# Turns before diagonal products in self-attention, and two row sends moved across a block's end

## The chip, the core and the metric

The kernel runs on one NeuronCore of a Trainium2 chip. The core has TensorE (matrix products; the profile shows its products as PE and its weight loads as PEld), VectorE (DVE), ScalarE (ACT), GpSimd (POOL) and SyncE (SP, which here only issues DMAs). The engines run side by side, each in the order of its own program, and meet on semaphores. The metric is the time of one execution on the device in microseconds (us), lower is better.

## The reference

A decoder layer over x of 32 batches x 100 tokens x 256 features, in float32, cut to what matters:

```python
x = x + attn(layernorm(x), wq, wk, wv, wo)        # 16 heads of 64, softmax over 100 keys, no mask
x = x + xattn(layernorm(x), context, mask, ...)   # 16 heads of 16, 361 keys
x = x + ffn(layernorm(x), centroids, w1, w2, ...) # 8 experts, one for each token

# self-attention, per head: the projection is *reshaped* to (heads, tokens, 64), not transposed
scores = softmax(q @ k.T * 64 ** -0.5)
out = (scores @ v).reshape(tokens, 1024) @ wo.T

# experts: eid = argmax(x @ centroids.T)
y = x + relu((xhat * gamma[e] + beta[e]) @ w1[e] + b1[e]) @ w2[e] + b2[e]
out = alpha * y + (1 - alpha) * x                 # alpha = sigmoid(x @ centroids[e])
```

## The kernel before

Four blocks follow each other: constants, self-attention (to 637 us), cross-attention (to some 1222 us) and the experts. A block ends when every engine has drained and met a barrier; GpSimd's drain and the barrier carry the line on which the block was opened or entered (L161 for self-attention, L847 for cross-attention).

**Self-attention.** Eight quads of four batches. A quad first projects queries, keys and values (the "body", TensorE lines L64 to L66), then runs eight rounds, r = 0 to 7, and three more (r = 8, 9, 10) in which the pipeline empties and the next quad's first projections are put between. A round takes two groups g of four heads, one of each of two batches. The softmax needs a maximum per query, so each score is computed twice. In round r TensorE does, in this order:

- L747: scores of round r, queries on the rows (4 loads), only for their maxima. VectorE reduces them to `row_max` (L634), GpSimd makes of each group's maxima a negative diagonal matrix `diag` (L541).
- L765: products of `probs` with the values for the groups of round r - 2 (16 loads, into `ps_o` and `ps_p`). `probs` is the weight operand, so the load itself waits for ScalarE's exponentials. VectorE then divides by the sums (L642, L646, `o_norm`).
- L787: scores of round r - 1 with the keys on the rows (16 small products into `ps_t`).
- L791: for each of the two groups one product of ones with `diag`, which subtracts the maxima in `ps_t` and completes it. ScalarE takes the exponentials after it (L454, `probs`).
- L801: four transposes, "turns", of `o_norm` of round r - 2 into `ps_ot`. ScalarE copies them out (L464, `stage`), GpSimd splits them in a high and a low part (L529 `o_hi`, L531 `o_lo`).
- after the fourth and the eighth round of outputs (in r = 6 and r = 10) the output products of two batches, 48 products on L64 to L66 that read `o_hi` and `o_lo` and wait for the last `o_lo`.

ScalarE's order in round r is: exponentials of round r - 1 (L454, each waits for its group's L791), copies of the turned outputs of round r - 2 (L464, wait for the turns of both groups), then the casts of the operands of round r + 2 (L275, L428). GpSimd's order in round r: the split of the outputs of round r - 3 (L529, L531), then the diagonals of round r, two of them, each of which may overwrite its buffer only after the L791 of the same buffer one round before. VectorE's: maxima, then `recip` and `o_norm` of the two groups, then the cast L275.

**The seam.** Cross-attention ends with the routing of the tokens to experts. Each batch's rows go to their places in `routed_rows` by an indirect DMA that GpSimd issues. For the last five batches (`LAST = 5`, batches 27 to 31) `send_last_rows` (L1225 to L1233) does it straight from `x`, by `last_slots`, which VectorE fills. In the end GpSimd does, for n = 29, 30, 31, `add_counts(n)` (L1196) and `send_last_rows(n - 1)`, then the send of batch 31, then waits for all landings (`routed`, L1295); SyncE waits for them as well (L1135), after it has issued the rows and weights of the experts' tiles 0 and 1.

**The experts.** 20 tiles of 256 or 128 rows. For tile 0: VectorE takes moments (L2195, L2199), GpSimd the roots (`roots(0)`, L2121 to L2125), VectorE `xhat` (L2206) and `feats` (L2211), GpSimd the sum `xf` (`residual(0)`, L2133), TensorE turns `xhat` (L2275), ScalarE makes `h_in` (L2167), TensorE the two layers (L2295, L2306). SyncE loads a tile's rows (L2032) and weights (L2037, L2038) two tiles ahead; the first that it loads in this block is tile 2, whose weights go to `w_third`. GpSimd scatters finished rows (L2140).

Of the kernel before, what the change touches and what calls it, by code (L numbers as in the profile page):

```python
# [25 lines left out]
GH = 4  # L26
# [24 lines left out]
HALVES = (2, 2, 2, 1) + (2, 2, 1) * 2 + (2, 1) * 5  # L51

EARLY_BATCHES = B - 6
EARLY = -(-(S * EARLY_BATCHES - E * (T - 1)) // T)
MAXT = (B * S + T - 1) // T
REGION = MAXT * T
# [98 lines left out]
def self_attention(nc, c, x, wqkT, wvT, woT, v_dram, xs, cross):  # L155
# [5 lines left out]
    with ExitStack() as ctx:  # L161
# [516 lines left out]
        def _(pe):  # L678
# [30 lines left out]
            def quad(q, last):  # L709
# [24 lines left out]
                for r in range(-1, ROUNDS + TAIL):  # L734
# [49 lines left out]
                    for h in range(GH):  # L784
                        for g in pair:

                            pe.matmul(ps_t[g % 2][0:S, S * h:S * (h + 1)], head(k_t, g, h), head(q_t, g, h),  # L787
                                      start=(h == 0), stop=False, skip_group_check=True)
                    for g in pair:
                        pe.wait_ge(diag_ready, q * GQ + (g + 1))  # L790
                        pe.matmul(ps_t[g % 2][0:S, 0:GH * S], c.ones_r[0:S, 0:S],  # L791
                                  diag[:, g % 2].rearrange("p h j -> p (h j)"), start=False, stop=True,
                                  skip_group_check=True).then_inc(shifted_ready, 1)
                    for g in in_round(r - 2):
                        pe.wait_ge(o_ready, q * GQ + (g + 1))
                        if g == 0:
                            reach(pe, x1_ready, q * QUAD)
                        if g >= 2:
                            pe.wait_ge(ot_copied_act, q * 2 * GQ + 2 * (g - g % 2))
                        for w in range(2):  # L800
                            ins = pe.transpose(ps_ot[:, 2 * S * (g % 2) + S * w:2 * S * (g % 2) + S * (w + 1)],  # L801
                                               o_norm[:, g % 2, 128 * w:128 * (w + 1)], c.ident[0:S, 0:S])
                        ins.then_inc(ot_ready, 1)
                    for g in in_round(r - 3):
                        if last_round_of_pair(r - 3):
                            i = batch_of(g)
                            pe.wait_ge(o_lo_ready, q * ROUNDS + (r - 2))
                            if i >= 2:
                                pe.wait_ge(x1_ready, q * QUAD + 2)
                            if isinstance(q, int) and q == 0:  # L810
                                pe.wait_ge(vo_lo_ready, 4)
                            hi, lo = (t[:, i % 2] for t in (o_hi, o_lo))
                            wo_hi, wo_lo = (w[:, 3].rearrange("p k n -> p (k n)").rearrange(
                                "p (t n) -> p t n", n=D) for w in (w_hi, w_lo))
                            for t in range(NT):
                                ins = split3(pe, ps_y[i // 2][0:S, D * (i % 2):D * (i % 2 + 1)], hi[:, t, :],
                                             lo[:, t, :], wo_hi[:, t, :], wo_lo[:, t, :], t == 0, t == NT - 1)
                            ins.then_inc(y_ready, 1)
# [14 lines left out]
def cross_attention(nc, c, ctxT, wo, bo, kb_dram, kd, qd, ones_dram, centT, xs, moe):  # L833
# [13 lines left out]
    with ExitStack() as ctx:  # L847
# [7 lines left out]
            return ctx.enter_context(nc.semaphore(name))  # L855

        KP = KT[0]
        LAST = 5
        wq_sb, wk_st, wv_st, wo_sb = c.wq_sb, c.wk_st, c.wv_st, c.wo_sb
        bq_sb, bk_sb, bv_sb, bo_sb, key_live = c.bq_sb, c.bk_sb, c.bv_sb, c.bo_sb, c.key_live  # L860
        wk_hi = sb("wk_hi", [128, KD, D], F32R)
# [46 lines left out]
        slot_f = sb("slot_f", [S, 1])  # L908
        slot = sb("slot", [S, 2], U32)
        last_f = sb("last_f", [S, 1])  # L910
        last_slots = sb("last_slots", [S, LAST], U32)
        ps_p = [psum(f"psb_p{i}", [128, 512]) for i in range(2)]
        ps_s = [psum(f"psb_s{i}", [128, 512]) for i in range(2)]
        ps_t = [psum(f"psb_t{i}", [128, 512]) for i in range(2)]
# [64 lines left out]
        counts_ready = sem("counts_ready")  # L979
        placing = sem("placing")  # L980
        slot_ready = sem("slot_ready")
        routed = [sem(f"routed{p}") for p in range(2)]
        last_placing = sem("last_placing")

        K0, Q0, K1, MT1, RT, V0, MT0, V1, V2, XT = range(10)
# [59 lines left out]
        def _(sp):  # L1045
# [85 lines left out]
            load_weights(sp, c, 0, c.w1_sb[:, 0], c.w2_sb[:, 0], moe["w1"], moe["w2"])  # L1131
            load_rows(sp, c, 1, xs)
            load_weights(sp, c, 1, c.w1_sb[:, 1], c.w2_sb[:, 1], moe["w1"], moe["w2"])
            for p in range(2):
                sp.wait_ge(routed[p], 16 * (B // 2))  # L1135

        @block.gpsimd
        def _(pool):
# [86 lines left out]
            def send_last_rows(n):  # L1225

                pool.wait_ge(slot_ready, n + 1)
                if n < EARLY_BATCHES + 2:
                    pool.wait_ge(routed[n % 2], 16 * (EARLY_BATCHES // 2))
                pool.indirect_dma_start(  # L1230
                    out=xs, out_offset=bass.IndirectOffsetOnAxis(ap=last_slots[:, n - (B - LAST):n - (B - LAST) + 1],
                                                                 axis=0),
                    in_=c.x[:, n, :], in_offset=None).then_inc(routed[n % 2], 16)  # L1233

            def routing(b, p):

# [52 lines left out]
            routing_root(B - 1)  # L1289
            for n in range(B - 3, B):  # L1290
                add_counts(n, n % 2)
                send_last_rows(n - 1)
            send_last_rows(B - 1)
            for p in range(2):
                pool.wait_ge(routed[p], 16 * (B // 2))  # L1295

        @block.scalar
        def _(act):
# [585 lines left out]

def table_buffers(nc, c, ctx):

    c.totals = ctx.enter_context(nc.sbuf_tensor("totals", [1, 2, E], F32))
    c.steps = ctx.enter_context(nc.sbuf_tensor("steps", [1, 3, MAXT], F32))
    c.tile_no = ctx.enter_context(nc.sbuf_tensor("tile_no", [1, BIG], F32))
# [142 lines left out]
    sp.dma_start(c.rows[:, j % 3, 0:nh], src).then_inc(c.rows_loaded[j % 3], 16)  # L2032


def load_weights(sp, c, j, w1_dst, w2_dst, w1, w2):
    e = expert_of(sp, c, j)
    sp.dma_start(w1_dst, w1[bass.ds(e, 1)].rearrange("o (k p) n -> p (o k) n", p=128)).then_inc(c.w_loaded[j % 3], 16)  # L2037
# [3 lines left out]
def experts(nc, c, xs, w1, w2, out):  # L2041
# [4 lines left out]
    with ExitStack() as ctx:  # L2046
# [56 lines left out]

        @block.sync
        def _(sp):
            for j in range(TILES - 2):
                if j + 2 == EARLY:
                    sp.wait_ge(c.tiles_ready, 6)
# [7 lines left out]
        def _(pool):  # L2116
# [26 lines left out]
                        oob_is_err=False).then_inc(scattered[j % 4], 16)  # L2143

            roots(0)
            residual(0)
            for j in range(TILES):
                if j + 1 < TILES:
# [252 lines left out]
```

## Time and profile before

| | |
|---|---|
| median of 3 runs | 1476.35 us (1476.33 to 1479.77) |
| the profiled execution | 1477.7 us, its span 1475.8 us, mean granted TensorE clock 0.977 |
| PE busy | 1372.4 us, 93% of the span |
| PEld busy | 1192.2 us, 81% |
| DVE / ACT / POOL busy | 950.5 (64%) / 761.4 (52%) / 651.4 us (44%) |
| DMA | 217.44 MB, mean 147 GB/s |
| self-attention, cross-attention, experts | 0 to 637, 637 to 1224.6, 1224.8 to 1475.8 us |

The span is the time from the first to the last instruction of the profiled execution; the device time has a little around it. A busy TensorE isn't one at its peak: products are pipelined and the ends of those in the profile are modelled, so the weight loads (PEld) show better when TensorE moves on. A row of the timeline gives start, length, engine, line, operation, output<-inputs, shapes and count; what stands in square brackets is the idle time of that engine before the row and the instruction that ended it. A q behind an engine's name marks its sequencer (waits, barriers, DMA issue).

### The profile page before, as it was taken

How to read it: one execution, taken by the hardware profiler on the slowest of the kernel's cores; microseconds unless marked ns; L12 is line 12 of the kernel's file. 1: busy time of each engine (PE TensorE's matmuls, PEld its weight loads, DVE VectorE, ACT ScalarE, POOL GpSimd, SP SyncE). 2: the span in 40 equal slices, each digit the busy share in tenths (PEclk: the TensorE clock that was granted, in tenths of full speed). 3: DMA queues.
4: the chain of work that ended last, by engine and by line, in shares of the span. 5: the costliest groups of instructions: out<-in, count | busy, mean ns of one | idle time of the engine just before them, and what ended most of it. 6: DMA issues, size and time to landing. Idle time of an engine off the chain costs nothing. (4 is left out here: it accounts for less than half of the span.)

```text
span 1475.8 us, 39048 instructions
## 1 busy us (share of the span) xinstructions
PE 1372.4 (93%) x12162; PEld 1192.2 (81%) x12162; DVE 950.5 (64%) x2409; ACT 761.4 (52%) x1882; POOL 651.4 (44%) x1001
## 2 busy tenths in 40 slices
PE   6999999999999999859999999999999976999997
PEld 5888888887878787847888888888888865888887
DVE  5757575757575666436777777777777754655554
ACT  5747474746565565514665656565565631222222
POOL 5534344352626171732345555555555541333332
PEclk9999999999999999978999999999999987999999
DMA  6607162524334252537767777677766652666662
GB/s 195 156 1 169 30 145 51 127 69 107 89 85 111 66 130 59 141 103 206 190 176 193 192 194 187 176 193 192 196 187 175 178 189 82 227 214 215 209 220 70
DMA packets 181116, 217.44 MB, mean 147 GB/s; under 512 B 83486, under 2 KB 148933, under 8 KB 180774
## 3 DMA queue, kind: packets, MB, share of 16 engines
q1 hardware_dynamic: 176424, 209.60, 52.2%
q0 software_dynamic: 3584, 6.58, 1.4%
q8 instruction: 44, 0.72, 0.2%
q10 hardware_dynamic: 1024, 0.21, 0.1%
q14 instruction: 40, 0.33, 0.1%
HBM read 137.62 MB, written 79.43 MB: 147 GB/s over the span
## 5 line engine op out<-in xcount | busy, mean ns | idle before, releaser
L1478 DVE TENSOR_REDUCE row_max<-psb_s 100x1 f32<-100x361 f32 x512 | 265.5, 530 | 143.5 <-PE psb_s L1694 137.8
L1348 ACT ACTIVATE probs<-psb_t 121x400 f32<-121x400 f32 (+1 forms) x384 | 190.5, 508 | 88.3 <-PE psb_t L1704 82.2
L541 POOL TENSOR_TENSOR diag<-neg_ident,row_max 100x400 fp32r<-100x400 f32 x128 | 112.9, 903 | 260.0 <-DVE row_max L634 231.3
L1694 PE MATMUL psb_s<-k,q 97*100 97x362 f32 x512 | 185.2, 364 | 15.3 <-DVE row_max L1478 7.7
L1704 PE MATMUL psb_t<-q,k 98*121 98x200 f32 (+1 forms) x768 | 146.4, 273 | 1.7 <-ACT probs L1348 1.7
L1704 PEld LDWEIGHTS psb_t<-q,k 98*121 98x121 f32 (+1 forms) x768 | 125.7, 184 | 4.5 <-ACT probs L1348 2.4
L454 ACT ACTIVATE probs<-ps_t 100x400 f32<-100x400 f32 x128 | 57.5, 501 | 113.2 <-PE ps_t L791 113.2
L1694 PEld LDWEIGHTS psb_s<-k,q 97*100 97x100 f32 x512 | 85.8, 168 | 35.5 <-DVE row_max L1478 18.0
L2181 ACT ACTIVATE hid<-psd_h,b_sb 128x256 f32<-128x256 f32 (+1 forms) x100 | 43.2, 432 | 113.7 <-PE psd_h L2295 113.6
L1717 PE MATMUL psb_o<-probs,v_ext 121*32 121x100 f32 (+1 forms) x3072 | 92.8, 253 | 0.0
L309 ACT COPY q_t<-ps_p 64x200 f32<-64x200 f32 x112 | 57.4, 512 | 63.6 <-PE ps_p L66 62.8
L529 POOL CAST o_hi<-stage 128x400 fp32r<-128x400 f32 x64 | 59.9, 937 | 62.0 <-ACT stage L464 33.5
L634 DVE TENSOR_REDUCE row_max<-ps_s 100x4 f32<-100x400 f32 x128 | 67.5, 570 | 28.7 <-PE ps_s L747 28.2
L2295 PE MATMUL psd_h<-h_in,w_sb 128*128 128x256 f32 (+1 forms) x448 | 83.1, 343 | 2.6 <-ACT h_in L2167 1.4
L464 ACT COPY stage<-ps_ot 64x200 f32<-64x200 f32 x256 | 81.7, 319 | 6.1 <-PE ps_ot L801 1.2
L64 PE MATMUL ps_p<-x_lo,w_hi 128*128 128x400 f32 x224 | 81.1, 362 | 4.0 <-DVE q_t L309 0.2
L531 POOL TENSOR_TENSOR o_lo<-stage,o_hi 128x400 fp32r<-128x400 f32 x64 | 81.7, 1277 | 5.1
L2295 PEld LDWEIGHTS psd_h<-h_in,w_sb 128*128 128x128 f32 x448 | 73.1, 195 | 11.7 <-DVE hid L2241 1.9
L1717 PEld LDWEIGHTS psb_o<-probs,v_ext 121*32 121x32 f32 (+1 forms) x3072 | 64.4, 110 | 21.4 <-issue 15.5
L2306 PE MATMUL psd_y<-w_sb,hid 128*128 128x256 f32 x352 | 80.4, 379 | 0.0
L66 PE MATMUL ps_p<-x_hi,w_hi 128*128 128x400 f32 x224 | 77.3, 345 | 0.0
L65 PE MATMUL ps_p<-x_hi,w_lo 128*128 128x400 f32 x224 | 76.9, 343 | 0.0
(255 smaller groups left out, 3738.1 us busy)
## 6 DMA issues: line engine op xcount, KB each, us to landing
w_sb<-in_w SPq DMA_DIRECT2D x28, 1024.0 KB, 7.5
routed_rows<-empty SPq DMA_DIRECT2D x7, 3855.0 KB, 19.8
packed_keys<-k_st SPq DMA_DIRECT2D x32, 724.0 KB, 4.4
k<-packed_keys SPq DMA_DIRECT2D x64, 362.0 KB
v_rows<-v_tok SPq DMA_DIRECT2D x32, 400.0 KB
v_ext<-v_rows SPq DMA_DIRECT2D x32, 400.0 KB
q<-packed_queries SPq DMA_DIRECT2D x64, 200.0 KB
w_third<-in_w SPq DMA_DIRECT2D x12, 1024.0 KB, 7.7
```

Source lines behind the costliest of these rows:

```text
L64: pe.matmul(out, hi_l, lo_r, start=first, stop=False)
L66: return pe.matmul(out, hi_l, hi_r, start=False, stop=last)
L464: act.copy(*turned_part(r - 2, a, odd)).then_inc(ot_copied_act, 1)
L531: pool.tensor_tensor(lo, src, hi.bitcast(F32), ALU.subtract).then_inc(o_lo_ready, 1)
L541: pool.tensor_tensor(diag[:, g % 2], c.neg_ident[0:S, 0:S].unsqueeze(1).to_broadcast([S, GH, S]), row_max[:, g // 2 % 2, g % 2].unsqueeze( ...
L1348: act.activation(probs[0:KT[kt], u % 2, kt], ps_t[i % 2][0:KT[kt], 0:4 * S], ACT.Exp, scale=HD2 ** -0.5).then_inc(probs_ready, 1)
L1478: dve.reduce_max(row_max[:, p, h:h + 1], ps_s[h % 2][0:S, 0:S2], AX_X).then_inc(max_ready, 1)
L1694: pe.matmul(ps_s[h % 2][0:S, 0:S2E], q2[0:97, p, u, g, S * a:S * (a + 1)], k2[0:97, p, u, g], start=True, stop=True).then_inc(scores_ready, 1)
L1704: ins = pe.matmul(ps_t[i % 2][0:n, 2 * S * g:2 * S * (g + 1)], k2[:, p, u, g, rows], q2[:, p, u, g], start=True, stop=True)
L1717: ins = pe.matmul(ps_o[32 * h:32 * (h + 1), S * u:S * (u + 1)], v_ext[0:n, p, kt, 4 * u + h, :], probs[0:n, u % 2, kt, S * h:S * (h + 1)], ...
L2295: ins = pe.matmul(ps_h[f % 4][:, 0:UNIT * nh], w1_sb[j % 3][:, k, 128 * f:128 * (f + 1)], h_in[:, j % 2, k, 0:UNIT * nh], start=(k == 0), ...
L2306: ins = pe.matmul(ps_y[n % 3][:, 0:D], hid[:, f, UNIT * t:UNIT * (t + 1)], w2_sb[j % 3][:, f, :], start=(f == 0), stop=(f == NF - 1))
```

## The change

Two parts. In self-attention the loop over the turns (L801) is placed ahead of the loop over the diagonal products (L791) in TensorE's program; nothing else of the round moves. At the seam the sends of batches 30 and 31 are taken out of the cross-attention block, with the waits for all landings on GpSimd and SyncE at its end; GpSimd issues them in the experts' block, after `roots(0)` and before `residual(0)`, and SyncE waits for all landings at the head of the experts' block, before it loads the rows of tile 2. `last_slots` and the two `routed` semaphores are allocated outside the block for that.

```diff
--- before.py
+++ after.py
@@ -51,6 +51,8 @@
 HALVES = (2, 2, 2, 1) + (2, 2, 1) * 2 + (2, 1) * 5
 
 EARLY_BATCHES = B - 6
+
+LAST = 5
 EARLY = -(-(S * EARLY_BATCHES - E * (T - 1)) // T)
 MAXT = (B * S + T - 1) // T
 REGION = MAXT * T
@@ -786,11 +788,6 @@
 
                             pe.matmul(ps_t[g % 2][0:S, S * h:S * (h + 1)], head(k_t, g, h), head(q_t, g, h),
                                       start=(h == 0), stop=False, skip_group_check=True)
-                    for g in pair:
-                        pe.wait_ge(diag_ready, q * GQ + (g + 1))
-                        pe.matmul(ps_t[g % 2][0:S, 0:GH * S], c.ones_r[0:S, 0:S],
-                                  diag[:, g % 2].rearrange("p h j -> p (h j)"), start=False, stop=True,
-                                  skip_group_check=True).then_inc(shifted_ready, 1)
                     for g in in_round(r - 2):
                         pe.wait_ge(o_ready, q * GQ + (g + 1))
                         if g == 0:
@@ -801,6 +798,11 @@
                             ins = pe.transpose(ps_ot[:, 2 * S * (g % 2) + S * w:2 * S * (g % 2) + S * (w + 1)],
                                                o_norm[:, g % 2, 128 * w:128 * (w + 1)], c.ident[0:S, 0:S])
                         ins.then_inc(ot_ready, 1)
+                    for g in pair:
+                        pe.wait_ge(diag_ready, q * GQ + (g + 1))
+                        pe.matmul(ps_t[g % 2][0:S, 0:GH * S], c.ones_r[0:S, 0:S],
+                                  diag[:, g % 2].rearrange("p h j -> p (h j)"), start=False, stop=True,
+                                  skip_group_check=True).then_inc(shifted_ready, 1)
                     for g in in_round(r - 3):
                         if last_round_of_pair(r - 3):
                             i = batch_of(g)
@@ -855,7 +857,6 @@
             return ctx.enter_context(nc.semaphore(name))
 
         KP = KT[0]
-        LAST = 5
         wq_sb, wk_st, wv_st, wo_sb = c.wq_sb, c.wk_st, c.wv_st, c.wo_sb
         bq_sb, bk_sb, bv_sb, bo_sb, key_live = c.bq_sb, c.bk_sb, c.bv_sb, c.bo_sb, c.key_live
         wk_hi = sb("wk_hi", [128, KD, D], F32R)
@@ -908,7 +909,7 @@
         slot_f = sb("slot_f", [S, 1])
         slot = sb("slot", [S, 2], U32)
         last_f = sb("last_f", [S, 1])
-        last_slots = sb("last_slots", [S, LAST], U32)
+        last_slots = c.last_slots
         ps_p = [psum(f"psb_p{i}", [128, 512]) for i in range(2)]
         ps_s = [psum(f"psb_s{i}", [128, 512]) for i in range(2)]
         ps_t = [psum(f"psb_t{i}", [128, 512]) for i in range(2)]
@@ -979,7 +980,7 @@
         counts_ready = sem("counts_ready")
         placing = sem("placing")
         slot_ready = sem("slot_ready")
-        routed = [sem(f"routed{p}") for p in range(2)]
+        routed = c.routed
         last_placing = sem("last_placing")
 
         K0, Q0, K1, MT1, RT, V0, MT0, V1, V2, XT = range(10)
@@ -1131,8 +1132,6 @@
             load_weights(sp, c, 0, c.w1_sb[:, 0], c.w2_sb[:, 0], moe["w1"], moe["w2"])
             load_rows(sp, c, 1, xs)
             load_weights(sp, c, 1, c.w1_sb[:, 1], c.w2_sb[:, 1], moe["w1"], moe["w2"])
-            for p in range(2):
-                sp.wait_ge(routed[p], 16 * (B // 2))
 
         @block.gpsimd
         def _(pool):
@@ -1227,10 +1226,7 @@
                 pool.wait_ge(slot_ready, n + 1)
                 if n < EARLY_BATCHES + 2:
                     pool.wait_ge(routed[n % 2], 16 * (EARLY_BATCHES // 2))
-                pool.indirect_dma_start(
-                    out=xs, out_offset=bass.IndirectOffsetOnAxis(ap=last_slots[:, n - (B - LAST):n - (B - LAST) + 1],
-                                                                 axis=0),
-                    in_=c.x[:, n, :], in_offset=None).then_inc(routed[n % 2], 16)
+                send_rows_of(pool, c, n, xs)
 
             def routing(b, p):
 
@@ -1289,10 +1285,8 @@
             routing_root(B - 1)
             for n in range(B - 3, B):
                 add_counts(n, n % 2)
-                send_last_rows(n - 1)
-            send_last_rows(B - 1)
-            for p in range(2):
-                pool.wait_ge(routed[p], 16 * (B // 2))
+                if n < B - 1:
+                    send_last_rows(n - 1)
 
         @block.scalar
         def _(act):
@@ -1884,6 +1878,8 @@
 
 def table_buffers(nc, c, ctx):
 
+    c.last_slots = ctx.enter_context(nc.sbuf_tensor("last_slots", [S, LAST], U32))
+    c.routed = [ctx.enter_context(nc.semaphore(f"routed{p}")) for p in range(2)]
     c.totals = ctx.enter_context(nc.sbuf_tensor("totals", [1, 2, E], F32))
     c.steps = ctx.enter_context(nc.sbuf_tensor("steps", [1, 3, MAXT], F32))
     c.tile_no = ctx.enter_context(nc.sbuf_tensor("tile_no", [1, BIG], F32))
@@ -2032,6 +2028,13 @@
     sp.dma_start(c.rows[:, j % 3, 0:nh], src).then_inc(c.rows_loaded[j % 3], 16)
 
 
+def send_rows_of(pool, c, n, xs):
+
+    at = n - (B - LAST)
+    pool.indirect_dma_start(out=xs, out_offset=bass.IndirectOffsetOnAxis(ap=c.last_slots[:, at:at + 1], axis=0),
+                            in_=c.x[:, n, :], in_offset=None).then_inc(c.routed[n % 2], 16)
+
+
 def load_weights(sp, c, j, w1_dst, w2_dst, w1, w2):
     e = expert_of(sp, c, j)
     sp.dma_start(w1_dst, w1[bass.ds(e, 1)].rearrange("o (k p) n -> p (o k) n", p=128)).then_inc(c.w_loaded[j % 3], 16)
@@ -2103,6 +2106,8 @@
 
         @block.sync
         def _(sp):
+            for p in range(2):
+                sp.wait_ge(c.routed[p], 16 * (B // 2))
             for j in range(TILES - 2):
                 if j + 2 == EARLY:
                     sp.wait_ge(c.tiles_ready, 6)
@@ -2143,6 +2148,8 @@
                         oob_is_err=False).then_inc(scattered[j % 4], 16)
 
             roots(0)
+            for n in (B - 2, B - 1):
+                send_rows_of(pool, c, n, xs)
             residual(0)
             for j in range(TILES):
                 if j + 1 < TILES:
```

## Rows read from the trace of the kernel before

**Rows 1.** Waits, 80 to 600 us: engine line waited for: us in total, times, longest.

```profile
PEld ps_o L765 <- ACT probs L454: 3.6, 14, 0.3
```

**Rows 2.** Timeline, fourth quad, a middle round and the start of the next.

```profile
289.54 0.82 PEld L765 LDWEIGHTS ps_o<-v_ext,probs 100*100 100x100 f32 x8
...
289.87 1.66 POOL L541 TENSOR_TENSOR diag<-neg_ident,row_max 100x400 fp32r<-100x400 f32 x2
...
291.46 0.42 DVE L646 TENSOR_TENSOR o_norm<-ps_p,recip 100x256 f32<-100x256 f32 x1
...
292.02 0.25 PEld L791 LDWEIGHTS ps_t<-diag,ones_r 100*100 100x100 f32 x2
292.29 0.49 PEld L801 LDWEIGHTS ps_ot<-ident,o_norm 100*128 100x128 f32 x4
...
292.48 0.90 ACT L454 ACTIVATE probs<-ps_t 100x400 f32<-100x400 f32 x2 [0.51 <-PE ps_t L791]
292.72 0.49 PEld L747 LDWEIGHTS ps_s<-k_pair,q_hi 128*100 128x100 f32 x4
293.16 0.81 PEld L765 LDWEIGHTS ps_o<-v_ext,probs 100*100 100x100 f32 x8
...
293.27 1.35 ACT L464 COPY stage<-ps_ot 64x200 f32<-64x200 f32 x4
...
293.72 1.67 POOL L541 TENSOR_TENSOR diag<-neg_ident,row_max 100x400 fp32r<-100x400 f32 x2
```

**Rows 3.** Timeline, the same quad, round 6 and its output products.

```profile
299.20 0.95 POOL L529 CAST o_hi<-stage 128x400 fp32r<-128x400 f32 x1
299.26 0.25 PEld L791 LDWEIGHTS ps_t<-diag,ones_r 100*100 100x100 f32 x2
...
300.22 1.24 POOL L531 TENSOR_TENSOR o_lo<-stage,o_hi 128x400 fp32r<-128x400 f32 x1
...
301.51 0.16 PEld L64 LDWEIGHTS ps_p<-w_lo,o_hi 128*100 128x100 f32 x1 [1.49 <-POOL o_lo L531]
```

**Rows 4.** Timeline, the same quad, the end of round 7 and the start of round 8.

```profile
309.97 0.42 DVE L646 TENSOR_TENSOR o_norm<-ps_p,recip 100x256 f32<-100x256 f32 x1
310.08 0.25 PEld L791 LDWEIGHTS ps_t<-diag,ones_r 100*100 100x100 f32 x2
...
311.10 0.25 PEld L765 LDWEIGHTS ps_o<-v_ext,probs 100*100 100x100 f32 x2 [0.26 <-ACT probs L454]
```

**Rows 5.** Lines L847, L161, L1230: ns min/median/max, first and last start.

```profile
L847 DVEq DRAIN  x1: 193/193/193, 1218.1 to 1218.1; - x1
L847 POOLq DRAIN  x1: 2686/2686/2686, 1221.8 to 1221.8; - x1
...
L161 POOLq DRAIN  x1: 1348/1348/1348, 627.2 to 627.2; - x1
...
DMA to landing us min/median/max: 2.8/4.5/6.4
```

**Rows 6.** Timeline at the seam and in the experts' first tiles.

```profile
1215.44 1.00 POOL L1230 DMA_INDIRECT routed_rows<-x_all,last_slots  x1 [0.71 <-DVE last_slots L1548]
1216.55 0.19 POOL L1196 TENSOR_TENSOR counts<-counts,onehot 100x8 fp32r<-100x8 f32 x1
...
1224.81 0.75 DVE L2195 BATCH_NORM_STATS2 stats<-stage 128x6 f32<-128x256 f32 x2 [6.57 <-PEq L847]
...
1226.57 0.38 SPq L2037 DMA_DIRECT2D w_third<-in_w  x1
...
1227.83 0.73 DVE L2206 TENSOR_SCALAR xhat<-stage,mv,rstd 128x256 f32<-128x256 f32 x2 [1.88 <-POOL rstd L2125]
...
1229.29 1.26 POOL L2133 TENSOR_TENSOR xf<-stage,feats 128x512 f32<-128x512 f32 x1 [1.50 <-DVE feats L2211]
...
1256.98 0.95 DVE L2211 TENSOR_SCALAR feats<-stage,mv,rstd 128x256 f32<-128x256 f32 x2
...
1263.26 4.29 PEld L2295 LDWEIGHTS psd_h<-h_in,w_third 128*128 128x128 f32 x20
```

**Rows 7.** Windows: us, busy by engine, PEclk (granted clock), DMA share, GB/s.

```profile
440.00:460.00 20.00, 18.68 (x188) 17.59 (x187) 12.83 (x37) 12.31 (x33) 16.39 (x18) 0.91 0.91 226
```

## The prediction, made before the change was built

> **What bounds the kernel now.** I read the page first, then a wait table of TensorE's side for the self-attention (it fills the first 637 us), then one round in order of time, then the seam between cross-attention and experts. TensorE is busy 93% of the span, so a step counts only where it makes TensorE wait. The wait table for 80 to 600 us has no entry in which TensorE waits for `diag`; it has one of 14 waits for `probs`, twice in each of seven quads [rows 1]. In a middle round, the fourth [rows 2], nothing on the weight-load row stands idle: from the load of one round's first L765 (289.54) to the next round's (293.16) are 3.62 us, all of it loads. GpSimd is busier than that: in a round it makes two diagonals (1.66 us [rows 2]), `o_hi` (0.95) and `o_lo` (1.24) [rows 3], 3.85 us, so it falls behind and TensorE waits 1.49 us for `o_lo` in round 6 [rows 3]. That gap is there in each quad.
>
> At the seam GpSimd stands on the path: it waits for its last sends to land, and its drain of 2686 ns starts only at 1221.8 [rows 5]; the experts' first instruction comes at 1224.81 with VectorE idle for 6.57 us [rows 6]. From there the tiles are a chain of TensorE work to the end.
>
> **Part 1, the turns (L801) ahead of the diagonal products (L791).** No instruction is added; the sum of loads on TensorE stays. What moves is the moment at which the exponentials can start. Now L791 starts at 292.02 and the turns at 292.29; the turns hold the row until L747 loads at 292.72, which is 0.43 us for four [rows 2]. After the change L791 starts 0.43 us later in every round that has turns (rounds 2 to 8).
>
> Who waits for L791: ScalarE's exponentials, started 0.46 us after it (292.48), and behind them the next round's L765, whose weights are `probs` [rows 2]. How long does L791 to L765 take when nothing else is between? Round 8 shows it: L791 at 310.08, L765 at 311.10 after an idle 0.26 us put down to `probs` [rows 4]: 1.02 us. In the middle round L765 comes 1.14 us after L791 (293.16 less 292.02), so only 0.12 us is spare. Taking 0.43 from it leaves a stall of 0.31 us, in rounds 3, 4, 5 and 6: 1.2 us. A round becomes 3.93 us. The cover that today hides the exponentials is just these turns.
>
> The turns themselves: they need `o_norm`. In a middle round the second one starts at 291.46 and takes 0.42, so it ends at 291.88, ahead of 292.02, and is only used by the third turn: no wait [rows 2]. In round 7, which starts late behind the output products, it ends at 309.97 + 0.42 = 310.39 while L791 starts at 310.08 [rows 4]; the third turn would come half of 0.43 after that, at 310.30, and waits until about 310.5, so 0.2 us more.
>
> Does TensorE's existing gap before round 6's output products (1.49 us) swallow the four stalls? Partly. They wait for GpSimd, and its chain starts from ScalarE's copies of the turned outputs, which stand behind the exponentials in ScalarE's queue: L464 at 293.27 follows the L454 pair of 292.48 [rows 2]. So the first copies come 0.43 us later, the fourth 0.43 + 3 x 0.31 = 1.36 us later. GpSimd was behind its copies by that round (it reached that `o_hi` at 299.20 [rows 3]; the copies, a round of 3.62 us after those of 293.27 and 1.35 us long [rows 2], ended at about 298.2, and `o_hi` follows copies it has waited for by some 0.25 us), so about 0.7 of the 1.36 is absorbed and `o_lo` lands 0.6 to 0.8 us later. I take 0.65 for a quad here; the bounds are 0.43 (GpSimd is the only limit and merely starts later) and 1.2 (nothing is absorbed).
>
> Then the tail of the quad. In round 8 and 9 L765 already waits for `probs` [rows 1, 4], so all of the delay counts: 0.43 + 0.2 in round 8, 0.43 in round 9, and nothing later in the quad makes it up, since `o_lo` of the last round is a chain from that L765. Per quad 0.65 + 0.63 + 0.43 = 1.71 us; eight quads are +13.7 us. Bounds: 8 x (0.43 + 0.86) = 10.3 and 8 x (1.2 + 1.06) = 18.
>
> Other queues: ScalarE has 0.51 us idle a round before its exponentials [rows 2] and shifts with them; a round's operands are cast two rounds ahead. GpSimd's diagonal may overwrite its buffer only after the L791 before the last: in the middle round that is 293.72 against 292.02 [rows 2], 1.7 us of room for 0.43. Nothing there is late next.
>
> **Part 2, the last two sends in the experts' block.** Removed: two sends of about 1.0 us on GpSimd, the wait for all landings on GpSimd and on SyncE before the block ends. GpSimd's last work in the block is then `counts` at 1216.55 + 0.19 [rows 6], and its drain can start at about 1216.8 in place of 1221.8: 5.0 us. The drain's 2.69 us stays: in the block before, where GpSimd had sent nothing, the drain of 1.35 us began while `o_lo` was still running [rows 5], but here it took 2.69 us with everything landed, so its length isn't the landings. Whether it can start before they have landed no row shows. If it can't, it starts after the landing of the send that remains (started at 1215.44 [rows 6], 4.5 us to landing in the median [rows 5], so 1220) and the gain is 1.8 us. I take the 5.0, since a drain that waited for landings would have had nothing left to wait for at 1221.8. VectorE is no limit: its drain starts at 1218.1 and takes 0.19 [rows 5].
>
> Added: in the experts' block GpSimd issues the two sends between its first roots and its first residual sum. They start at about 1227.8 on the old scale and take 2.3 us with the issue between them, so `xf` starts 1.0 us later than 1229.29 [rows 6]; it is read only when tile 0 is finished, some 20 us later. SyncE now waits at the block's head for these landings: old scale 1229.4 + 2.8 to 6.4 us [rows 5], then tile 2's rows and weights, whose weight issue moves from 1226.57 [rows 6] to some 1234 to 1238; landing takes about 8 us, and TensorE wants `w_third` at 1263.26 [rows 6]. That is 17 us spare, so nothing is late. On the path is only VectorE's `xhat` at 1227.83, now beside a send. Beside a scatter the two `feats` of 1256.98 took 0.95 us, where the like `xhat` pair of 1227.83 took 0.73 with nothing of GpSimd's beside it [rows 6], so I charge 0.2. Gain 4.8 us, bounds 1.6 and 5.0.
>
> The Trainium skill (SBUF — State Buffer, Who interferes with whom) says that a VectorE operation in a two-port mode and a GpSimd instruction lock each other out for the whole instruction. By it the second `xhat` could stand behind a send of 1.0 us and the gain would be about 3.9 us; the row with 0.22 us speaks for the smaller charge.
>
> **Sum.** +13.7 - 4.8 = +8.9 us. The profiled execution of before took 1477.7 us (span 1475.8), 1.35 us over the median of 1476.35. Against the median: 1485.3 us; the profiled span would be about 1484.7.
>
> **Rivals.** (a) *The turns cost nothing, and the kernel is faster.* GpSimd is behind: in round 6 its next `o_hi` starts at 299.20 and L791 at 299.26 [rows 3], so the second diagonal was ready with no margin. If it were 0.43 us later than the end of L787, the turns would fill a hole and cost nothing. Then only the seam is left: 1476.35 - 4.8 = 1471.5 us. Against it: no `diag` in the wait table, and in rounds 7 to 9 the diagonals are long done. (b) *Only the quad's tail pays.* If round 6's gap takes all of the stalls, and round 7's wait is nil, a quad costs 0.86 us: +6.9 - 4.8, 1478.5 us. Against it: ScalarE's queue order. (c) *The drain waits for the landings*: the gain is 1.6 us, so 1476.35 + 13.7 - 1.6 = 1488.5 us. (d) *The clock gives way.* The stretch 440 to 460 us stands at a mean granted 0.91 [rows 7]: a fall to the lower level (1.2 GHz) at one of the sixteen gaps before output products, worth some 20 x 0.09 = 1.8 us. With more small gaps in rounds 3 to 9 it might fall once in each quad: +8 x 1.8 = 14 us more, 1499 us. The Trainium skill (TensorE: Matmul & The Clock Gate, A second HAM failure mode: psum-queue depth-cycling) tells of such frequent micro-idles making the clock swing. Against it: rounds 8 and 9 of seven quads have two such gaps each today and the clock holds.
>
> **How the numbers follow.** Forecast 0.57 (own range 1482 to 1489); (a) 0.13; (b) 0.12; (c) 0.11; (d) 0.07. A measurement of this kernel tells about 0.3% (4.4 us) from no change. Slower by more than that is the forecast, (c) and (d), 0.75; (b) is within it, 0.12; (a) is faster, 0.13. The range leaves out (a) and (d) and reaches from (b) to beyond (c): 1477.5 to 1491.
>
> **What would show it.** Right: a new wait of L765 for `probs` of about 0.3 us in rounds 3 to 6 of each quad and of 0.7 to 0.9 in rounds 8 and 9; a round of about 3.93 us in place of 3.62; the gap before round 6's output products shrinking to about 0.9 us; a quad of about 1.7 us more; the experts' first instruction about 3.1 us after GpSimd's last `counts`; the first wait of tile 2 unchanged. Wrong: rounds still at 3.62 us, the drain starting after the landings, `xhat` a microsecond behind `rstd`, or a first row load of tile 2 that delays its moments.

## The result, and the profile after

| | before | after |
|---|---|---|
| median, 12 runs each | 1478.08 us (1474.77 to 1483.8) | 1483.12 us (1479.97 to 1484.8) |
| profiled execution, its span | 1477.7, 1475.8 us | 1484.8, 1482.4 us |
| mean granted TensorE clock | 0.977 | 0.974 |
| last output products of self-attention start | 628.5 us | 635.9 us |
| experts' first instruction | 1224.8 us | 1232.0 us |

The ratio is 1.003, with a 95% interval of 1.0017 to 1.0042: slower, by about 4.5 us, at the edge of what a measurement of this kernel can tell. (The median of before here is that of twelve runs, 1.7 us above that of the three shown ahead.)

Line numbers after are two or three higher on TensorE in the rounds (scores L749, products with the values L767, scores with the keys L789), the turns are L798 and the diagonal products L803. The wait table of TensorE's weight loads, 80 to 600 us (line waited for: us in total, times, longest), beside [rows 1]:

```profile
PEld ps_o L767 <- ACT probs L456: 14.0, 33, 0.8
PEld ps_p L66 <- POOL o_lo L533: 8.3, 6, 1.4
PEld ps_ot L798 <- DVE o_norm L648: 1.0, 6, 0.2
```

The 14 waits for `probs` of 3.6 us have become 33 of 14.0 us, and a wait for `o_norm` is new. (One more new wait of L767 a quad, 0.19 us in round 6, has the name "issue" in the same table.) The timeline shows the stalls one by one. A middle round of the fourth quad, beside [rows 2]:

```profile
291.60 0.37 PEld L798 LDWEIGHTS ps_ot<-ident,o_norm 100*128 100x128 f32 x4
...
291.92 0.25 PEld L803 LDWEIGHTS ps_t<-diag,ones_r 100*100 100x100 f32 x2
...
292.19 0.59 PEld L749 LDWEIGHTS ps_s<-k_pair,q_hi 128*100 128x100 f32 x4
...
292.39 0.90 ACT L456 ACTIVATE probs<-ps_t 100x400 f32<-100x400 f32 x2 [0.67 <-PE ps_t L803]
...
292.94 0.78 PEld L767 LDWEIGHTS ps_o<-v_ext,probs 100*100 100x100 f32 x8 [0.16 <-ACT probs L456]
...
296.73 0.34 PEld L767 LDWEIGHTS ps_o<-v_ext,probs 100*100 100x100 f32 x3 [0.17 <-ACT probs L456]
```

The idle 0.16 us ahead of L767 is new. From it to the next round's are 3.79 us, in place of 3.62. But the turns hold the diagonal products up by 0.32 us only (291.60 to 291.92), not by the 0.43 of [rows 2]. The same quad, the output products after the fourth round and then rounds 7 to 9, beside [rows 3, 4]:

```profile
304.90 0.16 PEld L66 LDWEIGHTS ps_p<-w_lo,o_hi 128*100 128x100 f32 x1 [1.37 <-POOL o_lo L533]
...
310.54 0.52 PEld L749 LDWEIGHTS ps_s<-k_pair,q_hi 128*100 128x100 f32 x4
...
313.48 0.20 PEld L798 LDWEIGHTS ps_ot<-ident,o_norm 100*128 100x128 f32 x2
313.83 0.20 PEld L798 LDWEIGHTS ps_ot<-ident,o_norm 100*128 100x128 f32 x2 [0.15 <-DVE o_norm L648]
313.98 0.25 PEld L803 LDWEIGHTS ps_t<-diag,ones_r 100*100 100x100 f32 x2
315.01 0.78 PEld L767 LDWEIGHTS ps_o<-v_ext,probs 100*100 100x100 f32 x8 [0.77 <-ACT probs L456]
...
318.14 0.37 PEld L798 LDWEIGHTS ps_ot<-ident,o_norm 100*128 100x128 f32 x4
318.45 0.26 PEld L803 LDWEIGHTS ps_t<-diag,ones_r 100*100 100x100 f32 x2
319.48 0.78 PEld L767 LDWEIGHTS ps_o<-v_ext,probs 100*100 100x100 f32 x8 [0.77 <-ACT probs L456]
```

From L803 to L767 are 1.02 to 1.03 us in the middle round and in rounds 8 and 9, as [rows 4] gave. The waits of rounds 8 and 9 are 0.77 us where they were 0.26.

At the seam, the lines of the block's end (ns min/median/max, first and last start) and of the sends, beside [rows 5], then the timeline, beside [rows 6]:

```profile
L849 POOLq DRAIN  x1: 4352/4352/4352, 1227.3 to 1227.3; - x1
...
L849 DVEq DRAIN  x1: 193/193/193, 1228.9 to 1228.9; - x1
...
L2034 POOL DMA_INDIRECT routed_rows<-x_all,last_slots x5: 994/1085/1184, 1219.4 to 1236.7; - x5
...
DMA to landing us min/median/max: 2.8/4.1/6.4
```

```profile
1226.27 1.00 POOL L2034 DMA_INDIRECT routed_rows<-x_all,last_slots  x1 [0.71 <-DVE last_slots L1542]
1227.38 0.19 POOL L1195 TENSOR_TENSOR counts<-counts,onehot 100x8 fp32r<-100x8 f32 x1
...
1232.04 0.75 DVE L2202 BATCH_NORM_STATS2 stats<-stage 128x6 f32<-128x256 f32 x2 [2.98 <-PEq L849]
...
1235.06 0.73 DVE L2213 TENSOR_SCALAR xhat<-stage,mv,rstd 128x256 f32<-128x256 f32 x2 [1.87 <-POOL rstd L2130]
1235.25 1.18 POOL L2034 DMA_INDIRECT routed_rows<-x_all,last_slots  x1 [0.23 <-issue]
...
1237.76 1.27 POOL L2138 TENSOR_TENSOR xf<-stage,feats 128x512 f32<-128x512 f32 x1
...
1241.44 0.38 SPq L2040 DMA_DIRECT2D w_third<-in_w  x1
```

GpSimd's drain now starts with its last `counts`, but takes 4.35 us, not 2.69. The send of 1226.27 is the one of the median landing time; it lands at 1226.27 + 4.1 = 1230.4, and the drain ends at 1231.7, 1.3 us later. `counts` ended at 1227.57, the experts start 4.47 us after it; before these were 8.07 us [rows 6].

**Where the time went.** From the start of one quad's last output products to the next quad's are 77.5 to 77.7 us after, 76.4 to 76.5 before in the quads without a fall of the clock, +1.17 us a quad, +9.3 in eight; the seam gives 3.6 back: +5.7, and 4.5 were measured. In the two profiled spans the difference is 6.6 us: the last output products of self-attention come 7.4 us later (9.3, less a fall of the clock that before has and after hasn't, less an earlier start), cross-attention up to its last `counts` is 3.5 us longer, the seam 3.6 shorter, the experts 0.6 shorter. Where the 3.5 us come from is only in part known. The code there is the same, and TensorE's clock is lower in the first 50 us of cross-attention: the windows below (us, busy by engine, then granted clock, DMA share, GB/s) have 0.74 before and 0.64 after. But in the profile of experiment e8 a clock of 0.65 in that stretch went with 1.2 us only, and e1, which has the rounds of after, took 0.6 us longer than before there. Over the thirteen profiles of this case the stretch takes 587.3 to 591.7 us, and after's is the longest.

```profile
630.00:680.00 50.00, 33.47 (x159) 27.72 (x158) 21.68 (x45) 9.91 (x25) 13.95 (x29) 0.74 0.54 146
```

```profile
637.00:687.00 50.00, 35.65 (x149) 29.71 (x148) 19.82 (x40) 8.49 (x21) 13.96 (x29) 0.64 0.54 146
```

### The profile page after: what moved, and what is told of

Same layout as the page of the kernel before. It is cut to its first block and busy times, and to the rows that moved or that the text cites. A ratio compares the mean times of both kernels' runs of the same rounds, so it can differ in the third digit from the quotient of the medians.

```text
span 1482.4 us, 39045 instructions
## 1 busy us (share of the span) xinstructions
PE 1381.9 (93%) x12162; PEld 1192.9 (80%) x12162; DVE 953.3 (64%) x2409; ACT 760.4 (51%) x1882; POOL 651.0 (44%) x1001
## 5 line engine op out<-in xcount | busy, mean ns | idle before, releaser
L67 PE MATMUL ps_p<-x_hi,w_lo 128*128 128x400 f32 x224 | 76.9, 343 | 0.0
```

## Experiments

A median of before stands beside each group of runs that shared it. "Quad" is again the time from one quad's last output products to the next quad's, in the profiled execution, without quads in which the clock fell.

### One half at a time (before 1477.66 us)

e1 takes the turns' new place alone, e2 the sends' alone.

```diff
@@ e1: before, TensorE's round @@
-  for g in pair: ... diag            # L791
   for g in in_round(r - 2): ... turns
+  for g in pair: ... diag
@@ e2: after, TensorE's round @@
-  for g in in_round(r - 2): ... turns
   for g in pair: ... diag
+  for g in in_round(r - 2): ... turns
```

> Only the turns (L801) ahead of the diagonal products (L791); the seam as before. Theory: the cost is the exponentials' latency, which the turns no longer hide. By the changed kernel's trace a middle round is 3.78 us (0.16 more), and a quad 0.33 us to the output products, 0.52 in round 7 to 8 and 0.32 in round 8 to 9: 8 x 1.17 = +9.4 us, ratio 1.0063. Rival (the sizes as predicted, and something else in the changed kernel gives 4 us back): +13.7 us, 1.0093. Rival (the turns cost nothing and the seam is what got slower): 0.

> Only the last two sends moved into the experts' block with the waits; rounds as before. Theory: GpSimd's drain lasts until the sends in flight have landed and some 1.3 us more, so from the last counts to the experts' first operation are 4.7 us (8.3 before): -3.6 us, ratio 0.9976. Rival (the drain has its fixed 2.7 us, as predicted): 3.1 us and -4.8 us, 0.9967. Rival (the wait comes back at tile 2's rows): 0.

e1: 1486.28 us, ratio 1.0057 (1.0038 to 1.0076), quad 77.6 us, the gaps of after in every round, the seam as before (8.2 us). e2: 1473.5 us, ratio 0.9969 (0.9952 to 0.9985), quad 76.4, first experts' instruction 3.39 us after `counts`. The interval of e1 holds the expected 1.0063 and leaves out both rivals. That of e2 holds both expected ratios; its trace lies between the 4.7 and the 3.1 us. The two ratios multiply to 1.0026, the whole change gave 1.0030: the halves add, the turns cost some 8.4 us and the sends save some 4.6.

### Turns ahead in some rounds only

e5 puts them ahead in rounds 2 to 6 (same runs of before as above), e6 in rounds 7 and 8 (before 1476.96 us).

```diff
@@ e5; in e6 the two conditions are r in (7, 8) and its opposite @@
+  for g in in_round(r - 2) if r <= 6 else (): ... turns
   for g in pair: ... diag
-  for g in in_round(r - 2): ... turns
+  for g in in_round(r - 2) if r > 6 else (): ... turns
```

> Turns ahead of the diagonal products in rounds 2 to 6 alone; rounds 7 and 8 and the seam as before. Theory of latency, with the gap ahead of the output products taking up half of the four stalls: 0.33 us a quad, +2.6 us, ratio 1.0018. Rival (no stall is absorbed: 4 x 0.16): +5.1 us, 1.0035. Rival (the gap absorbs all): 0.

> Turns ahead in rounds 7 and 8 alone, the seam as before. With e5 (rounds 2 to 6: +0.4 us a quad) and e1 (all: +1.17) the rest belongs to the tail: 0.2 for o_norm in round 7, 0.32 for round 8's wait, 0.32 for round 9's, 0.84 us a quad, +6.7 us, ratio 1.0045. If the terms don't add (the tail's wait partly covered when the quad arrives earlier), under +5 us. If the clock falls once in each quad as in e7, +16.

e5: 1480.07 us, ratio 1.0017 (1.0004 to 1.003), quad 76.8: +0.4. e6: 1485.82 us, ratio 1.0058 (1.0038 to 1.0079), quad 77.27: +0.85; its interval holds the expected 1.0045, and its profiled execution has two falls of the clock. The quads add, 0.4 + 0.85 against 1.2 in e1. The medians add less well: the two ratios multiply to 1.0075, and e1 gave 1.0057; the intervals leave room for that, and e6's two falls are worth some 3 us. So two thirds of the cost come from the two rounds of the tail. Rounds 2 to 6 lose a start 0.32 later and three stalls of 0.16 before the fourth round's turns, 0.80 us, and the gap before the output products takes half of that.

### One group's turns ahead

```diff
@@ e7: before, TensorE's round @@
+  for g in in_round(r - 2)[:1]: ... turns
   for g in pair: ... diag
-  for g in in_round(r - 2): ... turns
+  for g in in_round(r - 2)[1:]: ... turns
```

> Only the first group's two turns stand ahead of the diagonal products, the second group's behind them; seam as before. Theory of latency: the diagonal products start 0.16 us later and not 0.32; middle rounds have 0.12 to 0.16 us spare, so they stay at 3.62 to 3.66 us; rounds 8 and 9, which already wait, lose 0.16 each, and round 7 has no wait for the second group's o_norm: about 0.35 us a quad, +2.8 us, ratio 1.0019. Rival (a price of each turn that stands behind the small products, whatever the latency): half of +9.4, +4.7 us, 1.0032.

e7: 1489.01 us, ratio 1.007 (1.0046 to 1.0094), far beyond what was expected. The rounds did as forecast: middle rounds are back at 3.6 us without a wait, those of rounds 8 and 9 are 0.43. The excess is the clock. The window table of e7 (columns as above, the granted clock is the third from the end) has 5 us at the output products after each quad's fourth round; under it the same place in the sixth quad of before:

```profile
70.70:75.70 5.00, 4.00 (x34) 4.00 (x35) 1.37 (x8) 1.28 (x5) 3.81 (x5) 1.00 0.16 23
147.60:152.60 5.00, 3.98 (x21) 3.98 (x22) 1.31 (x8) 1.21 (x5) 3.83 (x5) 0.67 0.82 195
226.10:231.10 5.00, 4.00 (x21) 4.00 (x22) 1.33 (x8) 1.20 (x5) 3.80 (x5) 0.67 0.89 194
304.60:309.60 5.00, 4.04 (x22) 4.04 (x23) 1.30 (x7) 1.14 (x4) 3.77 (x5) 0.67 0.91 197
...
539.90:544.90 5.00, 4.05 (x22) 4.05 (x23) 1.29 (x7) 1.13 (x4) 3.76 (x5) 0.69 0.90 206
618.00:623.00 5.00, 3.76 (x32) 3.76 (x33) 0.00 (x0) 1.54 (x5) 2.81 (x3) 1.00 0.95 235
```

```profile
453.40:458.40 5.00, 3.99 (x21) 3.99 (x22) 1.45 (x8) 1.26 (x5) 3.81 (x5) 0.66 0.86 200
```

Six of eight quads (those left out read 0.68 and 0.69) have a fall to the lower level (1.2 GHz) there, where before has one. The timeline of e7's third quad shows the price:

```profile
227.10 0.16 PEld L64 LDWEIGHTS ps_p<-w_lo,o_hi 128*100 128x100 f32 x1 [1.73 <-POOL o_lo L531]
...
228.17 0.28 PEld L66 LDWEIGHTS ps_p<-w_hi,o_hi 128*100 128x100 f32 x1
...
234.26 0.52 PEld L747 LDWEIGHTS ps_s<-k_pair,q_hi 128*100 128x100 f32 x4
```

The 48 products take 7.16 us (227.10 to 234.26), 5.64 in the profile of after (304.90 to 310.54): 1.5 us a fall. Quads with one are 78.4 to 78.5 us long, the one without 76.9. Six falls, less the one of before, are 7.7 us, and eight quads longer by 0.5 are 4; together 11.7, and e7's span is 12.3 us over that of before.

The Trainium skill (TensorE: Matmul & The Clock Gate, A second HAM failure mode: psum-queue depth-cycling) describes another kernel whose clock swings because TensorE idles briefly and often. e7's trace agrees as far as each of its six falls stands behind a gap of 1.7 us. That the number of small gaps decides, the traces don't bear out: after, with 19 waits for `probs` more than before in the table above, has no fall before its last output products.

### The next quad's input turned first

Before and after turn the next quad's input (8 loads, 0.75 us) in round 8 behind L765. These kernels put it ahead of L765, into the wait for `probs`: e8 with the sends late (before 1478.17 us), e9 with the turns ahead (same), e11 with one group ahead (before 1476.96 us).

```diff
@@ TensorE's round @@
+  if r == ROUNDS and not last:
+      pe.wait_ge(max_ready, q * GQ + GQ)
+      turn_x(q + 1)
   for g in in_round(r - 2): ... products of probs with the values   # L765
-  if r == ROUNDS and not last:
-      pe.wait_ge(max_ready, q * GQ + GQ)
-      turn_x(q + 1)
```

> The seam as changed, the rounds as before, and in round 8 the eight transposes of the next quad's normalised input (0.87 us) ahead of L765 instead of behind it. Theory: L765's wait for probs of 0.26 us is covered in seven quads: -1.8 us beside the seam's -3.6: -5.4 us, ratio 0.9963. Rival (the wait is not latency of the exponentials, and stays): -3.6 us.

> Turns ahead of the diagonal products in all rounds, seam as before, and in round 8 the same eight transposes ahead of L765. Theory: L765's wait of 0.77 us there is time in which TensorE has nothing, so the 0.87 us of transposes cover it in seven quads: +9.4 - 5.4 = +4.0 us, ratio 1.0027. Rival (the turns' cost is TensorE's own work): +9.4 us, 1.0063.

> As e7 (only the first group's turns ahead of the diagonal products), and the turning of the next quad's input ahead of L765 in round 8, which fills that round's gap and makes a quad some 0.4 us shorter. Theory: the excess of e7 was only the fall of TensorE's clock once in each quad, at the gap before the output products, and hung on where the gaps lie; with another pattern of gaps the clock holds in nearly all quads, and the time is that of before plus 0.1 to 0.2 us a quad: +1 to +2 us, ratio 1.001, quad 76.5 us. Rival 1: the falls hang on the length of the gap before the output products alone (1.73 us in e7, 1.49 in before); then they recur in every quad, +9 us, ratio 1.006. Rival 2: one group ahead costs in itself; then the quads are long without a fall of the clock.

e8: 1471.49 us, ratio 0.9956 (0.9941 to 0.9971), quad 76.1, 0.3 less; the interval leaves out the rival's 0.9976. e9: 1482.43 us, ratio 1.0028 (1.0016 to 1.0039), quad 77.0; the interval leaves out the rival's 1.0063. Its timeline, fourth quad, rounds 7 to 9:

```profile
312.22 0.25 PEld L801 LDWEIGHTS ps_t<-diag,ones_r 100*100 100x100 f32 x2
312.50 0.83 PEld L689 LDWEIGHTS ps_s<-ident,xn 100*128 100x128 f32 x8
313.27 0.78 PEld L768 LDWEIGHTS ps_o<-v_ext,probs 100*100 100x100 f32 x8
...
317.06 0.78 PEld L768 LDWEIGHTS ps_o<-v_ext,probs 100*100 100x100 f32 x8 [0.77 <-ACT probs L454]
```

From L801 to the products with the values are 1.05 us in round 8, 0.03 more than with the idle time, and now the turning, which took 0.75 us behind L765, lies within. A quad is 0.63 us shorter than in e1 (76.99 against 77.62), so of the 0.77 us of round 8's wait at least 0.63 are on the path.

e11: 1481.34 us, ratio 1.003 (1.0015 to 1.0044), quad 76.4. Its windows at the same place in the third, fourth and seventh quad:

```profile
224.60:229.60 5.00, 4.44 (x25) 4.44 (x26) 1.38 (x4) 0.77 (x3) 3.37 (x5) 0.66 0.55 139
303.00:308.00 5.00, 4.89 (x41) 4.90 (x42) 1.39 (x4) 0.36 (x2) 2.91 (x5) 1.00 0.51 117
...
531.70:536.70 5.00, 4.43 (x24) 4.44 (x25) 1.39 (x4) 0.81 (x3) 3.37 (x5) 0.66 0.58 145
```

Two falls, not six, though TensorE waits as long before these output products as in e7 (10.4 us for six in both wait tables). So the first rival, that the gap's length alone decides, is out, and the second mostly: one group ahead costs 0.3 us a quad over e8, as the theory had it. But the median is 2 to 3 us above what the theory gave, so undisturbed clocks are not the rule either; its profiled span of 1476.5 us is among its shortest runs, and what the others did isn't seen.

### What the drain waits for (before 1478.17 us)

e3 leaves all five sends in the cross-attention block and moves only the waits for the landings to the experts. e4 sends four batches, 28 to 31, from the experts' block.

```diff
@@ e3: GpSimd, end of cross-attention and head of the experts @@
   for n in range(B - 3, B):
       add_counts(n, n % 2)
-      if n < B - 1:
-          send_last_rows(n - 1)
+      send_last_rows(n - 1)
+  send_last_rows(B - 1)
...
-  for n in (B - 2, B - 1):
-      send_rows_of(pool, c, n, xs)
@@ e4 @@
   for n in range(B - 3, B):
       add_counts(n, n % 2)
-      if n < B - 1:
-          send_last_rows(n - 1)
...
-  for n in (B - 2, B - 1):
+  for n in range(B - 4, B):
       send_rows_of(pool, c, n, xs)
```

(Both with the turns as before.)

> All five last sends stay in the cross-attention block, only the waits for landing go to the experts' block. Rounds as before. GpSimd's drain then starts about 1.1 us after the start of the last send, with three or four sends in the air. If the drain waits for them: it ends some 1.3 us after the last landing, so about 4 us long. If it is fixed: 2.7 us long.

> Four sends (batches 28 to 31) in the experts' block; rounds as before. Of the five only batch 27's is sent before the drain and has almost landed by then. If the drain waits for landings: it is under 2.7 us, and the seam gains 2 us more than with two sends moved: -5.6 us, ratio 0.9962. If it is fixed: 2.7 us, -4.8 us. On the other side the four sends hold GpSimd for 5 us between the roots and the residual sum, and tile 2's rows for as long; by the rows before neither is on the path.

e3, one run: 1474.66 us, too few for a verdict on its time; what counts here is its trace. Its drain, its last send and its landings:

```profile
L849 POOLq DRAIN  x1: 4602/4602/4602, 1217.2 to 1217.2; - x1
```

```profile
1217.71 0.99 POOL L2034 DMA_INDIRECT routed_rows<-x_all,last_slots  x1 [0.30 <-issue]
...
DMA to landing us min/median/max: 2.8/4.5/6.2
```

This send, the quickest, lands at 1220.5. The drain began 3.3 us before that, in the sequencer, and ended at 1221.8, 1.3 us after it. So it may start with transfers in the air, and then it waits for them. e4: 1470.91 us, ratio 0.9956 (0.994 to 0.9972):

```profile
L849 POOLq DRAIN  x1: 2621/2621/2621, 1214.3 to 1214.3; - x1
```

```profile
1214.31 0.20 POOL L1195 TENSOR_TENSOR counts<-counts,onehot 100x8 fp32r<-100x8 f32 x1 [1.82 <-DVE onehot L1519]
1217.26 0.75 DVE L2200 BATCH_NORM_STATS2 stats<-stage 128x6 f32<-128x256 f32 x2 [1.25 <-PEq L849]
```

The one send that it keeps had landed at 1212.6 (1206.3 + 6.3), and the drain took 2.62 us. The experts start 2.74 us after `counts`, and `w_third`, landed at 1237.6, is needed at 1255.8.

| | sends in the block | drain, us | its end after the last landing | `counts` to experts |
|---|---|---|---|---|
| before | 5, waited for | 2.69 | 2.9 | 8.07 |
| e3 | 5, not waited for | 4.60 | 1.3 | 6.50 |
| after | 3 | 4.35 | 1.3 | 4.47 |
| e8 | 3 | 4.53 | 1.3 | 4.65 |
| e2 | 3 | 3.27 | at most 1.7 | 3.39 |
| e4 | 1 | 2.62 | 4.3 | 2.74 |

The trace of e2 has no landing of its third send in the block; its second landed at 1217.3, and the drain ended at 1218.9.

### Both gains together (before 1476.96 us)

e10 is e4 with the input turned first, as in e8.

> Rounds as before, the sends of batches 28 to 31 in the experts' block, and the turning of the next quad's input ahead of L765 in round 8. The two gains lie in different blocks, so they should add: the seam of e4_four_sends_late (counts to the experts' first instruction 2.7 us in place of 8.1, -5.3 us) and the 0.3 us a quad of e8 (seven quads, -2.1 us): -7.4 us, ratio 0.995. Rival: run-to-run falls of the clock hide the 2 us and it stands level with e4, 0.9956.

e10: 1469.31 us, ratio 0.9943 (0.9928 to 0.9958), 7.7 us less than before, as the sum said; it beats both kernels. By the times alone the rival, level with e4, isn't excluded, since the intervals overlap; the trace has the shorter quad, 76.1 us. Its waits for `probs` in the same table:

```profile
PEld ps_o L770 <- ACT probs L456: 1.8, 7, 0.3
```

Half of [rows 1]: the seven of round 8 are filled, the seven of round 9 stay.

## Why the prediction was right, and where it was off

The forecast was 1485.3 us, own range 1482 to 1489; 1483.12 came out, within it (and within the 1477.5 to 1491 that the prediction also names). Against the +8.9 us of the sum, 4.5 to 5 were measured. The verdict, slower by about 0.3%, sits on the bound itself.

The mechanism was right, and the number was partly luck. Two errors of opposite sign met: the turns' part came out 4.4 us smaller than forecast, and the seam gave back 1.2 us less. And the base of the forecast, the median of three runs, was 1.7 us below that of the twelve; with 1478.08 the same sum gives 1487.0. Step by step:

- **Diagonal products later means exponentials later means L765 waits.** Right, in every round, and e1 alone shows it.
- **L791 to L765 takes 1.02 us when nothing hides it.** Right: 1.02 to 1.04 in rounds 3 to 6, 8 and 9 of the fourth quad of after.
- **The turns cost 0.43 us.** This is the term that was mis-sized: 0.32. In [rows 2] I took the time from the first turn's load to L747's as the price of four turns. There the turns follow the diagonal products, of 400 columns each, and whoever follows those holds the row for longer: L749's four loads hold the row for 0.75 us less a wait of 0.16, 0.59, where the like ones of [rows 2] take 0.44. The loads' own times tell it too: the turns 0.49 before and 0.37 after, L747 0.49 and 0.59. That the loads queue behind the wide products is my reading of this; no run shows the queue itself. With 0.32 the stall becomes 0.32 - 0.12 = 0.20 us; it measured 0.16. Rounds 8 and 9 come to 0.52 and 0.32 in place of 0.63 and 0.43, and that is what they cost: from round 8's L767 to round 9's are 4.47 us (315.01 to 319.48) where the profile of before has 4.15.
- **`o_norm` holds the third turn by 0.2 us in round 7.** Right: 0.15 of idle.
- **The gap before the output products takes part of the stalls.** Right in kind. With the smaller terms the copies come 0.32 + 3 x 0.16 = 0.80 us later; the output products came 0.33 later, against 0.65 forecast, so 0.47 was absorbed and not 0.7. The gap went from 1.49 to 1.37, not to 0.9. GpSimd was less far behind than I had read from [rows 3].
- **A quad of +1.71.** It was 0.33 + 0.52 + 0.32 = 1.17: +9.3 us and not +13.7. These 4.4 us are the miss; the seam's 1.2 us work against them, and the 1 us that is left is within the spread of the runs.
- **The seam, -4.8.** In the profile of after it was -3.6. The step that failed is the drain's fixed 2.69 us. It does start with the last `counts`, so rival (c) had the wait at the wrong end, but its end waits for the landings: it took 4.35 us, to 1.3 us after the last. The inference that a drain which waits for landings "would have had nothing left to wait for" took 2.69 for a length that landings can't stretch; 2.62 to 2.69 us are the least that was seen in this block, with everything landed. The other support, the drain of 1.35 us at the end of self-attention, didn't bear on it: that drain ended with `o_lo`, the last work of GpSimd there. e2 had -4.7 with a drain of 3.27 us, so with one slow landing more or less the gain moves between 3.4 (e8) and 4.7.
- **0.2 us for `xhat` beside a send.** None: 0.73 us for the two, the first send starting 0.19 after them. The Trainium skill (SBUF — State Buffer, Who interferes with whom) has a VectorE operation in a two-port mode and a GpSimd instruction exclude each other for a whole instruction. If `xhat` runs in that mode, which no run here shows, the second one could have come a send later; the trace has no such delay at this place.
- **Tile 2 has 17 us to spare.** Right: `w_third` landed at 1249.6 and was used at 1270.1, 20 us.
- **Rivals.** (a) fell with e1: the second diagonal is no hole that turns could fill. (b), only the tail pays, had the tail right (0.86 forecast, 0.85 in e6), but rounds 2 to 6 pay 0.4 more (e5), and the seam gives less. (d), the clock falls once in each quad, didn't happen in the change's kernel but in e7, a smaller dose of it, at the price that it was given (1.5 us a fall, 1.8 forecast).

Open is what makes the clock fall after one such gap and not after another. Gaps of 1.7 us had falls behind them in six of eight quads in e7 and in two of eight in e11; gaps of 1.5 us had one in before, at 454.4, one in e3, at the same place, and two in e6. The length of the gap doesn't decide: before the second output products of a quad TensorE waits 1.7 us in every kernel, and no profile has a fall at one of these waits but at the end of the last quad, where the wait is 4.0 us. In the fourth quad of before:

```profile
323.04 0.17 PEld L64 LDWEIGHTS ps_ot<-w_lo,o_hi 128*100 128x100 f32 x1 [1.71 <-POOL o_lo L531]
```

```profile
322.00:327.00 5.00, 3.96 (x33) 3.96 (x34) 0.72 (x2) 1.63 (x4) 0.99 (x1) 1.00 0.00 0
```

What decides wasn't found.

## What to carry to other kernels

Price a moved block by what it delays at its new place: here four turns held the row for 0.43 us behind products of 400 columns and for 0.32 behind products of 100, and the wait they left behind goes to whoever follows the wide products next. Before moving a step past another, look who waits for the one that becomes later; where that wait already exists in some rounds, all of the delay lands there, and independent work (here the next quad's input) is what should fill it. At a block's end, keep indirect DMAs that GpSimd issued out of its last microseconds: in three profiles its drain waited for them, to 1.3 us after the last landing, though no instruction of the block did.

## What the runs showed that I had not expected

GpSimd's drain at the end of the cross-attention block took 2.62 to 2.69 us when all its indirect transfers had landed, and otherwise until 1.3 us after the last landing (three profiles). At the end of self-attention, where it had issued none, its drain of 627.2 took 1.35 us [rows 5] and ended within 0.1 us of its last work:

```profile
627.24 1.24 POOL L531 TENSOR_TENSOR o_lo<-stage,o_hi 128x400 fp32r<-128x400 f32 x1
```

Why the drain behind the sends takes 2.6 us even when they have landed stays open.

TensorE's clock fell to its lower level in most passes of a loop after a tiny change of order: in six quads of eight in e7, at 1.5 us each, two thirds of what that change cost. A single profile of before has one such fall, so a difference of 1 to 2 us between two kernels' spans here is no evidence until the windows with less than 1.00 of granted clock are counted.
